# Attention times values in pairs of key tiles: one stretch per two loop steps

## The reference

```
c_kv  = x @ W_dkv.T
q_lat = einsum('bqhd,hdl->bhql', x @ W_dq.T @ W_uq.T, k_eff)
attn  = softmax(causal(einsum('bhql,bkl->bhqk', q_lat, c_kv) / sqrt(hs)))
y     = einsum('bhql,hld->bqhd', einsum('bhqk,bkl->bhql', attn, c_kv), v_eff)
x     = layernorm(x + y)
x     = layernorm(x + experts(x))     # top-2 routing, relu(x @ wi) @ wo
```

## Time and profile before

| | before |
|---|---|
| median of three runs | 616.11 us |
| span of the profiled execution | 613.6 us |
| TensorE busy | 523.1 us (85%) |
| VectorE busy | 447.6 us (73%) |
| ScalarE busy | 349.4 us (57%) |
| GpSimd busy | 63.1 us (10%) |
| `attn_v` matmuls (L1056) | 1280 records, 146.9 us busy |

### The profile page before, as it was taken

How to read it: one execution, slowest core, us unless ns; L and a number is a source line. 1 busy time by engine, 2 the same in 40 slices (tenths; PEclk the granted TensorE clock), 3 DMA queues, 4 the chain that set the end, 5 groups by cost and what they waited for, 6 DMA issues and landing times.

```text
span 613.6 us, 10353 instructions
## 1 busy us (share of the span) xinstructions
PE 523.1 (85%) x3445; PEld 220.9 (36%) x3491; DVE 447.6 (73%) x1311; ACT 349.4 (57%) x751; POOL 63.1 (10%) x64
## 2 busy tenths in 40 slices
PE   5762679998999998898999999999999988856990
PEld 3420333333433333323445433333233221223790
DVE  4771669989899898885766889989889833337616
ACT  0700445665677676475665677667777779920230
POOL 9300000000000000071000270000000000000031
PEclk9955879999999999999999999999999999995996
DMA  3579800812000001211000151000000000000024
GB/s 105 142 175 222 190 11 2 256 49 50 2 2 2 1 2 40 41 53 39 2 12 2 25 48 10 1 3 1 0 2 2 2 1 10 28 0 1 0 44 49
DMA packets 25362, 24.90 MB, mean 41 GB/s; under 512 B 2266, under 2 KB 22620, under 8 KB 25308
## 3 DMA queue, kind: packets, MB, share of 16 engines
q1 hardware_dynamic: 24028, 21.60, 14.1%
q0 software_dynamic: 1280, 2.62, 3.5%
HBM read 16.81 MB, written 7.28 MB: 39 GB/s over the span
## 4 chain that ended last, share of the span: by engine, by line
PE 50%; issue 20%; DVE 12%; DMA 7%; SPq 4%; ACT 4%; POOL 3%; DVEq 0%; ACTq 0%; POOLq 0%
PE acc L1056 15%; PE sc L1018 13%; PE scT L1039 11%; DMA parts_k<-wi 4%; DVE unused L752 3%; POOL exp_in L558 2%; SPq L452 2%; ACT probs L627 2%; DVE part_max L747 2%; DMA qT<-maxT 2%; PE scT L1043 2%; PE ms L1141 2%; PE ms L1147 1%; DVE kT L907 1%; SPq L441 1%
## 5 line engine op out<-in xcount | busy, mean ns | idle before, releaser
L627 ACT ACTIVATE probs<-scT 128x512 f32<-128x512 f32 (+3 forms) x640 | 302.7, 540 | 140.0 <-PE scT L1043 84.4
L747 DVE TENSOR_REDUCE part_max<-sc 128x1 f32<-128x512 f32 x384 | 249.9, 685 | 25.5 <-PE sc L1018 22.3
L1018 PE MATMUL sc<-kT,qT 126*128 126x512 bf16 (+3 forms) x640 | 224.0, 362 | 19.0 <-DVE part_max L747 7.7
L1039 PE MATMUL scT<-qT,kT 128*128 128x512 bf16 (+3 forms) x594 | 202.1, 350 | 5.8 <-ACT probs L627 4.3
L752 DVE CUSTOM_DVE_ANT_0 unused<-sc,causal 128x128 bf16<-128x128 f32 (+3 forms) x256 | 120.9, 484 | 48.1 <-PE sc L1018 46.5
L1056 PE MATMUL acc<-probs,v 128*9 128x512 f32 (+3 forms) x1280 | 146.9, 532 | 0.4
L1018 PEld LDWEIGHTS sc<-kT,qT 126*128 126x128 bf16 x640 | 62.7, 99 | 149.4 <-DVE part_max L747 82.4
L1039 PEld LDWEIGHTS scT<-qT,kT 128*128 128x128 bf16 x640 | 62.3, 99 | 78.7 <-ACT probs L627 32.4
L1043 PE MATMUL scT<-later,ident 128*128 128x128 bf16 x256 | 56.2, 222 | 19.7 <-DMA qT<-maxT 19.1
L1056 PEld LDWEIGHTS acc<-probs,v 128*9 128x9 f32 x1280 | 19.2, 88 | 47.5 <-ACT probs L627 33.9
L1043 PEld LDWEIGHTS scT<-later,ident 128*128 128x128 bf16 x256 | 25.7, 100 | 19.9 <-issue 0.9
(11 more groups left out here) (182 smaller groups left out, 338.4 us busy)
## 6 DMA issues: line engine op xcount, KB each, us to landing
kT<-parts_k SPq DMA_DIRECT2D x9, 384.0 KB
qT<-parts_q SPq DMA_DIRECT2D x9, 384.0 KB
wi<-in_L_ffn_wi SPq DMA_DIRECT2D x1, 2048.0 KB, 8.5
parts_k<-wi SPq DMA_DIRECT2D x3, 384.0 KB, 9.3
parts_q<-wi SPq DMA_DIRECT2D x3, 384.0 KB, 8.2
kT<-parts_k SPq DMA_DIRECT2D x6, 192.0 KB
qT<-parts_q SPq DMA_DIRECT2D x6, 192.0 KB
x<-in_L_attn_x SPq DMA_DIRECT2D x4, 256.0 KB, 3.8
```

The lines of the kernel that those rows point to most:

```text
L627: nc.scalar.activation(probs[n % PRING][:, 0:width], scT[n % SRING][:, 0:width], ACT.Exp).then_inc(exp_done, 1)
L747: nc.vector.tensor_reduce(dst, sc[i % SRING][:, :], AX.X, ALU.max).then_inc(sc_used, 1)
L1018: nc.tensor.matmul(sc[i % SRING][:, 0:w], qT[s % 2][0:MROW, head, qt * P:(qt + 1) * P], kT[0:MROW, head, c * QUERIES:c * QUERIES + w], sta ...
L1039: ins = nc.tensor.matmul(scT[n % SRING][:, 0:QUERIES - off], kT[:, head, j * P:(j + 1) * P], qT[s % 2][:, head, off:QUERIES], start=True, ...
```

## The change

Two steps' `attn_v` are issued in one stretch at the end of every even loop step, and none at the end of an odd one. LAG goes from 2 to 1, so that at even b the stretch holds `attn_v(b-2)` and `attn_v(b-1)`. The first of the two stands where it stood; the second stands one loop step earlier than it did. All units have an even number of steps, so no pair crosses a unit. `keep_y` moves one loop step ahead on ScalarE. The instructions themselves are the same in number and shape, and VectorE's stream is unchanged.

```diff
-LAG = 2
+LAG = 1
+BATCH = 2
...
+assert all(unit_steps(_u) % BATCH == 0 for _u in range(UNITS))
...
-                if LAG <= b < NSTEP + LAG:
-                    attn_v(b - LAG)
+                if LAG <= b < NSTEP + LAG and (b - LAG) % BATCH == BATCH - 1:
+                    for step in range(b - LAG - BATCH + 1, b - LAG + 1):
+                        attn_v(step)
```

## The result

The changed kernel takes 635.75 us (median of four runs, 635.13 to 636.44), the kernel before 616.8 us in the same comparison: 1.031 times as long, 95% interval 1.0295 to 1.0327. Forecast were 633.1 us and 17 us more; it became 19. The span of the profiled execution went from 613.6 to 633.6 us.

The account below looks back on a forecast made before the run. TensorE was taken to bound the item steps, VectorE having a tenth of a step in reserve. Terms were summed to 18.7, less 1.7 gave +17: span 613.6 to 630.6, plus 2.5 outside it, 633.1 us; range 623 to 643.

Parts of the forecast that it names:

- The plain pair: Two ordinary steps with items: VectorE idle 1.06 us, 6.04 against 5.66 (+0.38), or 5.84 against 5.55 (+0.29).
- The pair with `max_turn`: Transposes at the odd step, no longer covered by a stretch, wait for VectorE: +0.7 us, half in supers 0 and 1.
- Around a unit's end: Three pairs around a unit's end, narrow then wide: together +0.8 us.
- Unit 15: Unit without items: ScalarE starved over the stretch, 5.22 against 4.74 us a pair (+0.48); five full pairs, 2.2 us.
- Experts: Steps 70 to 85, where VectorE has slack: eight pairs gain 0.2 us each, -1.6 us.
- Units 4 to 11: Units 4 to 7 lose 1.3 us each, 5.2; units 8 to 11 lose 3.6 after the expert pairs' deductions.
- a term of -1.7 us: Steps 16 to 69: part of the loss disappears in TensorE's idle time, mostly behind layer norm and routing chains; -1.7 us.
- unit 12: Two pairs of each plain kind 1.34, max_turn 0.7, unit's end 0.8: +2.8 us.
- The worse one: Rival: the second half of a stretch does not run on, 642 us; chance 0.13.
- The faster one: Rival: saved switches, 0.20 us in each of 80 pairs, 600 us; chance 0.03 full, 0.03 in part (605 to 614).
- The third: Rival, no change: plain pairs lose half as much, experts and narrow pairs give it back; 616 us, chance 0.04.
- The fourth: Rival, half the loss: VectorE's step-end tasks fill its idle time over the stretch; 618 to 625 us, chance 0.10.

Follow-up runs that it names:

- e1: Changed kernel with one attn_v stretch per step again, so only the lag differs from the kernel before: 615.68 us against 616.14, ratio 0.9989.
- e8: Changed kernel with max_turn one step later for units 2 to 15, behind the paired stretch: 637.40 us, ratio 1.0311 to the kernel before.
- e4: Changed kernel with VectorE's work cut, row maxima of full items taken over 128 of 512 columns: 601.16 us.
- e10: Changed kernel with row maxima over 128 of 512 columns and single stretches in unit 15 and at selected other pairs: 590.37 us, ratio 0.9561 to the kernel before.
- e9: Kernel before with paired stretches only at steps 70, 72, 74, 76, 78, 82 and 84: 616.32 us against 615.69, ratio 1.0001.
- e7: Kernel before with paired stretches only at steps 70, 72, 74, 76, 78, 82, 84, 142, 158 and 160: 617.84 us against 617.01, ratio 0.9992.
- e2: Kernel before with paired stretches only at the even expert steps 70 to 84: 615.73 us against 616.14, ratio 0.9975.
- e3: Kernel before with VectorE's work cut, row maxima of full items taken over 128 of 512 columns: 601.77 us, ratio 0.9769.
- e5: Changed kernel with a single stretch in every step of unit 15 (steps 144 to 159): 635.82 us, ratio 1.0293 to the kernel before.
- e6: Changed kernel with single stretches in steps 103 to 106, around a layer norm chain: 634.08 us, ratio 1.0252 to the kernel before.

## Why the prediction was right

**The mechanism** held as forecast: work unchanged, no wait from the lag (e1), the second half of a stretch running on (16 records in 1.91 us), VectorE idle over it. Forecast were 1.06 us of idle time before the first item and 1.06 were measured.

**The plain pair** was put at 6.04 and 5.84 us and measured at 5.95 and 5.77: +0.30 and +0.22 in place of +0.38 and +0.29. The idle time was right; VectorE's work was 0.08 too high. I took 0.69 us for a masked item from steps in which the next item was not there yet. With a full queue the next reduction starts together with the small read of the accumulator (both at 462.61), and only one of the two reads of a pair is paid for.

**The pair with `max_turn`**: +0.60 from stretch to stretch, forecast +0.7. After, the last score, the maxima and the transposes (compare):

```profile
467.05 0.38 PE L1041 MATMUL scT<-qT,kT 128*128 128x512 bf16 x1
...
467.66 0.16 DVE L770 TENSOR_TENSOR max<-neg_max,max 128x16 bf16<-128x16 f32 x1
...
467.97 0.38 PE L1027 MATMUL ms<-ident,max 128*8 128x128 bf16 x4 [0.54 <-DVE max L770]
468.28 0.10 PEld L1020 LDWEIGHTS sc<-kT,qT 126*128 126x128 bf16 x1
468.29 0.23 PE L1020 MATMUL sc<-kT,qT 126*128 126x128 bf16 x1
```

The next item comes 1.24 us behind the score, forecast 1.31, before 1.49. But e8 shows that half of this term is not the wait's own: it overlaps with the starvation, and taking the wait away alone brings back 0.4.

**Around a unit's end**: +0.82 over three pairs (0.22, 0.38, 0.22), forecast +0.8. **Unit 13** as a whole: +2.5, forecast +2.8.

**Unit 15** with the tail: +2.9, forecast +2.2. The plain pairs there were right (+0.44 from stretch to stretch, forecast 0.45 to 0.48); the layer norm's two operations on ScalarE, 0.23 and 0.21 us, were left out of the chain.

**Experts**: seven of eight pairs are 0.17 to 0.28 us shorter, the one with `max_turn` 0.3 longer, together -1.3; forecast -1.6.

**Units 4 to 11.** Units 4 to 7: +5.1, forecast +5.2. Units 8 to 11: +2.2, forecast +3.6. The forecast had beside these a term of -1.7 us, for idle time behind chains in steps 16 to 69 in which part of the loss would disappear. With it the steps 16 to 96 were put at 7.1, and 7.2 were measured. But the agreement is luck. The chains did not hide the loss: the pairs at 56, 58 and 60, with chains through VectorE, were 0.91, 0.85 and 0.64 us longer. What did hide a part was a wait for a DMA ahead of the pair at 70, which was 1.4 us shorter: TensorE, being later itself, stood idle there for 1.44 us in place of 2.79.

```profile
292.01 0.63 PE L1116 MATMUL ms<-ident,back 128*128 128x128 f32 x4 [1.44 <-DMA back<-exp_in]
```

**What failed** is the same idea in unit 12, where the forecast had no term for the chain at all. I expected that VectorE's waits in a chain would, if anything, hide part of the loss. They made it larger: each link has an item ahead of the next, and an item that is late holds up the chain (the row at 409.81). Steps 102 to 108 take 4.2 us more than before; by e8, about 1.5 of it is the clock and the rest the chain and the missing stretch. So unit 12 lost 5.2 us in place of 2.8. Units 13 and 14 came as forecast (2.5 and 1.9 for 2.8 and 1.9), and the three together lost 9.6 and not 7.5.

**The sum** in the prediction is wrong by 0.4: its terms add up to 19.1 and not 18.7, so that with the -1.7 it should have said +17.4. From step 6 on the traces have +21.1. Of the missing 3.7, units 12 to 14 are 2.1, unit 15 0.7, and units 0 to 3 another 0.7 (+1.3 from step 6 to 16, forecast 0.6 in all), which no run explains. That the start was 1.0 us shorter in the changed kernel's trace brought the span closer to the forecast by chance.

**The rivals.** The worse one (the second half late, 642) is out by the 16 records. The faster one (600) named the right saving, 0.21 us a pair in e4. Its condition was too strict: it asked that VectorE never run dry over the stretch, but in e4 VectorE is idle for 1.68 us and the pair still gains. What counts is whether VectorE's work and its idle time together stay below TensorE's own time for the pair. The third (no change) is out by the time and by +0.30 a plain pair, where it needed half of my 0.38. The fourth (VectorE's tasks done over the stretch) is out by the time and by the chain rows. On the weight loads the trace of the changed kernel repeats what the one of before said: weights for the same rows of the array load at 458.38 while matmuls run.

`attn_v` fell from 146.9 to 131.9 us busy, more than the 10 forecast, and says nothing of the time: it is how the overlap of records is counted.

## What to carry to other kernels

When a matmul stretch feeds no consumer, compare its length with the work in the consumers' queues, at the moment when the last item is issued. Here the queue held 1.76 us and the next item came 2.82 us later. Then add the idle time to the consumer's work for the whole pair, and compare with the producer's own time: by the forecast 4.98 + 1.06 us on VectorE against 5.46 on TensorE. The larger one sets the pair, and a saving of 0.2 us on the busiest engine turned into a loss of 0.3 us. Saved switches are real, and can be had where the consumers have slack or where the producer has other work anyway; look for these places one by one, by stage, and leave the others as they are.

## What the runs showed of the hardware that was not expected

- TensorE's granted clock fell from full to half (from 2.4 to 1.2 GHz) in the loop steps of 8 of the 12 traces, in one place each, for 3.4 us (in e10 for 6.8). At step 69 it fell in or behind idle times of 3.01 to 4.18 us (e9, e7, e2, e4, e10, e3) and not with 1.24 to 2.79 (changed kernel, e5, e6, e8, e1, before). At step 105 it fell behind 2.39 us in the changed kernel and in e5, and not behind the same 2.39 in e8. So the idle time alone does not decide it here, and no run shows what does. The 3.4 us cost 1.5 to 1.6: the pair at 106 takes 9.74 us in the changed kernel and 8.26 in e8; the one at 70 takes 10.54 in e2 against 8.55 before, of which 0.4 is the longer wait. Some of the scatter between runs of one kernel may come from it: in the comparison in which the kernel before took 614.48 to 621.88 us, its two slowest runs have the lowest mean clock of all 23 (0.934, the others 0.940 to 0.950). But in another one a slow run (621.99) has a clock like the fast ones (0.945), so this is not all of it.
- A read of VectorE's accumulator (0.08 us) runs beside the next reduction if that one's input is there (462.61), and is paid for if not.
- The cost of going from bf16 scores to the four-column-group matmuls and back was 0.09 + 0.11 us by the rows of before and 0.21 by e4.
